# Quantizing the second weight of a two-layer kernel: one piece a tile over 32 tiles instead of two over 16, scaled on ScalarE

## The reference, cut to what matters

```python
x = x + _L0_ffn_ref(_L0_cond_ref(x, L0_cond_weights, itok_B_0_15), ...)   # first layer
x = x + _L1_ffn_ref(_L1_cond_ref(x, itok_B_6_15, ...), ...)               # second layer

# inside _L1_ffn_ref: both operands are rounded to float8 before the product
x_q = _quant_fp8(x, 1.0 / input_scale)
w_q = _quant_fp8(weight, 1.0 / weight_scale)      # weight: 1024 x 1024, (w * scale_inv).astype(float8_e4m3fn)
acc = jnp.einsum('ni,io->no', x_q.astype(jnp.float32), w_q.astype(jnp.float32))
out = acc * (input_scale * weight_scale) + bias
```

## Time and profile before

| | us |
|---|---|
| median of 3 runs | 2068.76 (2067.19 to 2071.76) |
| the profiled execution | 2070.12 |
| its span on the core | 2068.3 |
| PE busy in the span | 2022.6 (98%) |
| DVE busy | 1438.4 (70%) |
| POOL busy | 517.7 (25%) |
| ACT busy | 381.3 (18%) |

### The profile page before, as it was taken

How to read it: one execution, slowest core, us unless ns; L and a number is a source line. 1 busy time by engine, 2 the same in 40 slices (tenths; PEclk the granted TensorE clock), 3 DMA queues, 4 the chain that set the end, 5 groups by cost and what they waited for, 6 DMA issues and landing times.

```text
span 2068.3 us, 36401 instructions
## 1 busy us (share of the span) xinstructions
PE 2022.6 (98%) x11969; PEld 1898.7 (92%) x12032; DVE 1438.4 (70%) x3786; ACT 381.3 (18%) x1052; POOL 517.7 (25%) x470
## 2 busy tenths in 40 slices
PE   7998999999999999999999999999999999999998
PEld 6998999999999999999988888888888888888887
DVE  6798987555555555555557777777777777777777
ACT  3111111111111111111111221211211211211211
POOL 3654411111111111111112222222322322222322
PEclk8999999999999999999999999999999999999999
DMA  7753443333333333333354556556556556556553
GB/s 237 238 172 118 140 125 103 93 107 107 96 93 111 106 94 93 113 105 93 93 175 145 157 154 168 160 157 166 159 161 164 157 164 163 155 168 159 155 170 112
DMA packets 220193, 289.85 MB, mean 140 GB/s; under 512 B 97795, under 2 KB 169477, under 8 KB 220166
## 3 DMA queue, kind: packets, MB, share of 16 engines
q1 hardware_dynamic: 220166, 289.56, 48.4%
HBM read 163.62 MB, written 109.05 MB: 132 GB/s over the span
## 4 chain that ended last, share of the span: by engine, by line
PE 90%; DVE 7%; issue 1%; SPq 1%; DMA 1%; ACT 0%; DVEq 0%; ACTq 0%
PE bank_g L946 12%; PE bank_g L948 12%; PE bank_g L947 12%; PE bank_g L1000 12%; PE bank_g L999 12%; PE bank_g L998 11%; PE bank_f L1008 10%; PE bank_t L929 5%; PE bank_g L1043 1%; PE bank_g L973 1%; PE bank_g L974 1%; PE bank_g L975 1%; DVE hwt L317 1%; DVE wq_pow L751 1%; DVE x1buf L812 1%
## 5 line engine op out<-in xcount | busy, mean ns | idle before, releaser
L946 PE MATMUL bank_g<-w0h,st_h 128*128 128x384 f32 (+1 forms) x1536 | 525.5, 342 | 18.6 <-DVE x1buf L812 15.3
L948 PE MATMUL bank_g<-w0h,st_l 128*128 128x384 f32 (+1 forms) x1536 | 524.0, 341 | 0.0
L947 PE MATMUL bank_g<-w0l,st_h 128*128 128x384 f32 (+1 forms) x1536 | 523.7, 341 | 0.0
L998 PE MATMUL bank_g<-w1h,st_h 128*128 128x352 f32 x1536 | 506.6, 330 | 2.9 <-DVE st_l L863 2.5
L1000 PE MATMUL bank_g<-w1h,st_l 128*128 128x352 f32 x1536 | 497.3, 324 | 0.0
L999 PE MATMUL bank_g<-w1l,st_h 128*128 128x352 f32 x1536 | 496.4, 323 | 0.0
L863 DVE TENSOR_TENSOR st_l<-xbuf,st_h 128x512 fp32r<-128x512 f32 x128 | 213.2, 1708 | 186.6 <-ACT st_h L663 186.6
L552 POOL TENSOR_TENSOR xbuf<-xbuf,b_base_sb 128x1024 f32<-128x1024 f32 x64 | 153.7, 2402 | 704.2 <-PE bank_t L929 690.7
L946 PEld LDWEIGHTS bank_g<-w0h,st_h 128*128 128x128 f32 x1536 | 292.0, 190 | 21.7 <-DVE st_l L711 17.0
L998 PEld LDWEIGHTS bank_g<-w1h,st_h 128*128 128x128 f32 x1536 | 289.6, 189 | 11.0 <-DVE st_l L863 2.8
L947 PEld LDWEIGHTS bank_g<-w0l,st_h 128*128 128x128 f32 x1536 | 291.6, 190 | 0.0
(11 more groups left out here) (79 smaller groups left out, 2085.6 us busy)
## 6 DMA issues: line engine op xcount, KB each, us to landing
xbuf<-x SPq DMA_DIRECT2D x64, 512.0 KB, 3.8
x_scratch<-x1buf SPq DMA_DIRECT2D x64, 512.0 KB, 2.9
x1t_scratch<-x_blocks SPq DMA_DIRECT2D x256, 128.0 KB, 2.2
xbuf<-x1t_scratch SPq DMA_DIRECT2D x64, 512.0 KB, 3.6
x1buf<-x_scratch SPq DMA_DIRECT2D x64, 512.0 KB, 5.1
out<-obuf SPq DMA_DIRECT2D x64, 512.0 KB, 2.7
b_stack<-b_split SPq DMA_DIRECT2D x384, 64.0 KB, 3.5
raw<-a_split SPq DMA_DIRECT2D x128, 128.0 KB, 4.1
```

Of the source, the lines that this page charges most:

```text
L946: pe.matmul(to, st_h[:, rows], w0h[:, k, cols], start=(k == 0), stop=False)
L947: pe.matmul(to, st_h[:, rows], w0l[:, k, cols], start=False, stop=False)
L948: last = pe.matmul(to, st_l[:, rows], w0h[:, k, cols], start=False, stop=(k == KC - 1))
L998: pe.matmul(to, st_h[:, rows], w1h_k[:, k, cols], start=(k == 0), stop=False)
```

## The change

The number of pieces a tile goes from two to one, and the tiles that carry one are now 2 to 33; the piece stands at the end of VectorE's tile, after the transpose, and none before `st_lo(n, 0)`. The first of the seven instructions, the multiplication by `inv_w`, becomes a ScalarE instruction, in place in `wq_val`, after that tile's `st_hi`; VectorE waits for `wq_scaled`. SP's `feed(t)` no longer alternates: it feeds GpSimd's pieces first, and then reloads the weight's buffer for the piece of the tile before. The tiles written out grow from 18 to 34 for SP, GpSimd and VectorE; ScalarE's were written out for 2 and now are for 34.

```diff
-PREP_TILES = 18
-WQ_TILES = range(2, 18)
-WQ_A_TILE = 2
 WQ_COLS = 256
 WQ_PIECES = D * D // P // WQ_COLS
-WQ_STEPS = 7
+WQ_FIRST_TILE = 2
+WQ_STEPS = 6
+PREP_TILES = WQ_FIRST_TILE + WQ_PIECES
...
+def wq_piece(t):
+    return t - WQ_FIRST_TILE if WQ_FIRST_TILE <= t < PREP_TILES else None
...
                 def feed(t):
-                    quantized = [*wq_pieces(t - 1)[WQ_A_TILE - 1:], *wq_pieces(t)[:WQ_A_TILE - 1]]
-                    for n, u in zip_longest(pool_pieces(t), quantized):
+                    for n in pool_pieces(t):
                         feed_pool(n)
-                        feed_wq(u)
+                    feed_wq(wq_piece(t - 1))
...
-                tile(0, True)
-                tile(1, True)
-                with act.Fori(2, TILES - 3, 2) as i:
+                def scale_weight(u):
+
+                    act.wait_ge(wq_loaded[u % 2], 16 * (u // 2 + 1))
+                    val = wq_val[:, u % 2, :]
+                    act.activation(val, val, ACT.Copy, scale=inv_w[:, :]).then_inc(wq_scaled, 1)
+
+                for t in range(PREP_TILES):
+                    tile(t, True)
+                    if t == WQ_FIRST_TILE:
+                        act.wait_ge(s_scale, 3)
+                    if wq_piece(t) is not None:
+                        scale_weight(wq_piece(t))
+                with act.Fori(PREP_TILES, TILES - 3, 2) as i:
...
-                    dve.wait_ge(wq_loaded[u % 2], 16 * (u // 2 + 1))
-                    dve.tensor_scalar(val, val, inv_w[:, :], None, ALU.mult).then_inc(wq_step, 1)
-                    dve.wait_ge(wq_step, base + 1)
+                    dve.wait_ge(wq_scaled, u + 1)
                     dve.tensor_scalar(power.bitcast(U32), val.bitcast(U32), 0x7F800000, None, ALU.bitwise_and)\
                        .then_inc(wq_step, 1)
...
                     move_hw(dve.tensor_copy, 1)
-                    for u in wq_units[0:1]:
-                        quantize_weight(u)
-                    for u in wq_units[1:WQ_A_TILE - 1]:
-                        quantize_weight(u)
                     if more:
                         st_lo(n, 0)
...
-                    for u in wq_units[WQ_A_TILE - 1:]:
-                        quantize_weight(u)
+                    if piece is not None:
+                        quantize_weight(piece)
```

More of the change, by code:

```diff
@@ L14 @@
 from contextlib import ExitStack
-from itertools import zip_longest
 import numpy as np
@@ L62 @@
 OVERFLOW_C = float(np.float32(2.0 ** 127 / 235.0))
-PREP_TILES = 18
-WQ_TILES = range(2, 18)
-WQ_A_TILE = 2
 WQ_COLS = 256
 WQ_PIECES = D * D // P // WQ_COLS
-WQ_STEPS = 7
+WQ_FIRST_TILE = 2
+WQ_STEPS = 6
+PREP_TILES = WQ_FIRST_TILE + WQ_PIECES
 POOL_PIECES_A_TILE = 3
-def wq_pieces(t):
-    first = WQ_A_TILE * (t - WQ_TILES[0])
-    return range(first, min(first + WQ_A_TILE, WQ_PIECES)) if t in WQ_TILES else ()
+def wq_piece(t):
+    return t - WQ_FIRST_TILE if WQ_FIRST_TILE <= t < PREP_TILES else None
 def build(nc, x, ids0, ids1, wc, m0, b0, b_base, w1t, base_bias, a1, b1, wf, bias2, s_in, s_w, out):
@@ L205, in build @@
             wq_loaded = [sem(f"wq_loaded{b}") for b in range(2)]
+            wq_scaled = sem("wq_scaled")
             wq_step = sem("wq_step")
@@ L738, in quantize_weight, with tile @@
                     base = WQ_STEPS * u
-                    dve.wait_ge(wq_loaded[u % 2], 16 * (u // 2 + 1))
-                    dve.tensor_scalar(val, val, inv_w[:, :], None, ALU.mult).then_inc(wq_step, 1)
-                    dve.wait_ge(wq_step, base + 1)
+                    dve.wait_ge(wq_scaled, u + 1)
                     dve.tensor_scalar(power.bitcast(U32), val.bitcast(U32), 0x7F800000, None, ALU.bitwise_and)\
                        .then_inc(wq_step, 1)
+                    dve.wait_ge(wq_step, base + 1)
+                    dve.tensor_scalar(power, power, MIN_NORMAL, ROUND_C, ALU.max, ALU.mult).then_inc(wq_step, 1)
                     dve.wait_ge(wq_step, base + 2)
-                    dve.tensor_scalar(power, power, MIN_NORMAL, ROUND_C, ALU.max, ALU.mult).then_inc(wq_step, 1)
+                    dve.tensor_tensor(val, val, power, ALU.add).then_inc(wq_step, 1)
                     dve.wait_ge(wq_step, base + 3)
-                    dve.tensor_tensor(val, val, power, ALU.add).then_inc(wq_step, 1)
+                    dve.tensor_tensor(to, val, power, ALU.subtract).then_inc(wq_step, 1)
                     dve.wait_ge(wq_step, base + 4)
-                    dve.tensor_tensor(to, val, power, ALU.subtract).then_inc(wq_step, 1)
+                    dve.tensor_scalar(wq_nan, to, OVERFLOW_C, 0.0, ALU.mult, ALU.mult).then_inc(wq_step, 1)
                     dve.wait_ge(wq_step, base + 5)
-                    dve.tensor_scalar(wq_nan, to, OVERFLOW_C, 0.0, ALU.mult, ALU.mult).then_inc(wq_step, 1)
-                    dve.wait_ge(wq_step, base + 6)
                     dve.tensor_tensor(to, to, wq_nan, ALU.add).then_inc(wq_step, 1)
-                def tile(t, b, stored, blocks, more, wq_units=()):
+                def tile(t, b, stored, blocks, more, piece=None):
                     n = t + 1
@@ L822, in tile @@
                                   x1buf[:, b, :].rearrange("p (k q j) -> p k q j", q=4, k=KC)).then_inc(blocks_done, 1)
-                    for u in wq_units[WQ_A_TILE - 1:]:
-                        quantize_weight(u)
+                    if piece is not None:
+                        quantize_weight(piece)
                 for t in range(PREP_TILES):
-                    tile(t, t % 2, 16 * (t // 2) if t >= 2 else None, 64 * t if t else None, True, wq_pieces(t))
+                    tile(t, t % 2, 16 * (t // 2) if t >= 2 else None, 64 * t if t else None, True, wq_piece(t))
                 with dve.Fori(PREP_TILES, TILES - 3, 2) as i:
```

## The result

The changed kernel takes 2044.99 us (median of 4 runs, 2044.25 to 2045.61), the one before 2070.26 beside it (2067.19 to 2072.36). The ratio is 0.9875, with a 95% interval of 0.9863 to 0.9887: faster by 25.3 us. The profiled execution took 2044.62 us, its span is 2042.8, against 2070.12 and 2068.3.

The account below looks back on a forecast made before the run. PE bounds the kernel, losing time only to VectorE stalls and slow clock in tiles 2 to 17. Idle 15.3 plus slow clock 7.7 make 23.0 us, off 2068.76: 2045.8 us; range 2043.0 to 2054.0.

Parts of the forecast that it names:

- The sum: Tiles 2 to 17: 22.99 us excess goes, 15.3 of PE idle and 7.7 at the lower clock; nothing added on the path.
- The late piece: VectorE after the transpose: six steps put `negmax` at +5.7 or +6.4, `hwt` at +12.3 or +13.0 against +14.5; cost 0.
- the +7.9: Latest `negmax` after a tile's first bank matmul, 14.5 - 6.6; past it beside wide splits the prediction is wrong.
- its upper bound: Worst traced piece, tile 3's before `st_lo`, put late: `negmax` +8.1, `hwt` +14.7, 0.2 us late; under 1 us over four tiles.
- a fraction of a us: SP's `feed(t)` may pass 15.89 us by this in tiles 2 to 5; costed at 0, upper bound 1 us.
- Rival A: Full exclusion: late piece can't run beside any split, `hwt` 2.8 us late in four tiles; about 2059 us; whole or part 0.13.
- The stated slack: Room before `hwt` is needed at +14.5: 2.2 us beside narrow splits, 1.5 beside wide ones; PE waits for nothing.
- The scaling: Multiplication moved to ScalarE after `st_hi`: 0.42 us, result near +0, VectorE asks at +2.7; costs 0.
- the early piece: VectorE's piece ahead of `st_lo(n, 0)`, held to be what is late: 4.73 us in tile 9, 5.79 in tile 3; removed.
- The reading of L751: VectorE's L751 takes 2.34 us in tile 9 against 0.23 in tile 15, standing until GpSimd's bias addition ends.
- The added tiles: Tiles 18 to 33 gain a piece of 2.05 us, hidden before the first bank group ends at +4.8; cost 0.
- Rival C: SP's late weight reload holds ScalarE's scaling and the exponential behind it; at 1.0 us a tile, 2078 us; chance 0.04.

## Why the prediction was right, and where it wasn't

The predicted 2045.8 us lies 0.8 from the measured 2045.0, and the range held it. Part of that closeness is luck. The forecast takes 23.0 us off a median of 2068.76, and beside the changed kernel the kernel before took 2070.26: 23.0 us were forecast and 25.3 measured. That no tile stalls at all is also partly luck, as tile 6 shows below.

**The sum.** 22.99 us were to go between tiles 2 and 17; 22.95 went, idle and slow clock both. The rest of the 25.3 is behind the first layer and in the spread of the runs. That stretch took 1022.7 and 1022.5 us in the two profiles of the kernel before, and 1020.1 to 1022.4 in the eleven of the other kernels, all with the same second layer. The difference between two of those is nearly as large as what is to be explained. Part of it is the landing of one small transfer into `b_stack`, for which PE waited 1.95 us before and not at all after; but the runs with the longer piece and with the added wait, both below 1021.3, waited 1.96 and 2.04 for it. Another part is the clock: over the 80 us behind the last `cond` the mean granted clock is 0.96 in both profiles of the kernel before, and 0.98 to 1.00 in the other eleven. The prediction had named a change of the second layer's time as a sign that it is wrong, and there is one, of 2.7 us. Whether the change has a share in it is open; the prediction saw no cause, and the runs show none.

**The late piece.** `negmax` at +5.7 beside narrow splits was right (+5.8). Beside wide ones +6.4 was right for tiles 3 and 4 (+6.1 and +5.9) and wrong for 5 (+7.3), and tile 6, whose splits are narrow, has +8.1. That is past the +7.9 that the prediction named as a sign of being wrong beside wide splits, and it is its upper bound for `negmax` to the tenth; it had taken 0 and not that bound. Two steps failed. One is SP's: its backlog of "a fraction of a us" was costed at nothing because what it loads is early. But it delays GpSimd's splits, the splits delay the bias addition, and the addition then meets the late piece. The other is the price of six steps beside wide splits, "some 3.7", from one tile: the run with two splits a tile has 4.73 with no addition beside them. Rival A had the exclusion at the splits alone and for the whole piece. The runs show it step by step, at the splits and, longest, at the addition. The stated slack of 2.2 or 1.5 us was 0 in tile 6. It cost 0.04 us here. With pieces longer by 1.3 us, tile 6 alone lost 6.2 of the 8.3 us.

**The scaling.** 0.42 us was estimated, 0.50 measured, off the path as said. That it is worth little where it stands was true of the changed kernel (about 2 us, 2046.95 against 2044.99, of which 1.3 are in the tiles with splits). But alone it brings 21 of the 25 us, with two stalls left, in tiles 4 and 6. The prediction gave the whole gain to the early piece, and didn't add up VectorE's chain. That chain is, with the addition kept away, 15.8 us to `st_lo`, against 14.4. Without the scaling the early piece is 0.4 us shorter (171.42 - 169.38 = 2.04 after 177.78 - 175.34 = 2.44) and the late one, beside splits, 0.7; the chain of that kernel ends at +14.5 (171.42 less 156.88), a tenth from what is wanted. Taking the early piece out removes 2.4. From tile 8 on either is enough, and together they don't add.

**The lock.** The reading of L751 held: it starts 0.11 us after the addition and ends 0.09 us after it, and L749 stands in the same way in tile 6 of the changed kernel, until 0.15 us after the addition's end. The Trainium skill, "SBUF — State Buffer", section "SBUF: two separate sides", has the engine that starts first keep the shared port pair for its whole instruction, where the VectorE instruction is in a mode that uses two ports or has two inputs in SBUF. The rows of the addition agree (2.37 and 2.34 us for steps of 0.29 and 0.23); those of a split's first instruction don't, as the last section shows. `st_lo`, which has one of its inputs in `bank_t`, where TensorE writes, takes its usual 0.68 in tile 8 of the kernel with the scaling alone moved, where it starts at 171.42 and the addition at 171.61. The collision makes a small lateness large: `st_lo` would be 1.0 us late in tile 9 of the kernel before and is 3.3 late (202.21 less 184.51, against +14.4). Which tiles it strikes differs between two executions.

**The added tiles.** 714.90 us from tile 17 to the last `cond`, before and after, with 16 more pieces in it: 0, as costed. Rival C doesn't occur: ScalarE is never idle before its 32 scalings, so the reload of a piece is never waited for.

## What to carry to other kernels

Add up the fixed-order queue of the engine that is late, from the event that starts it to the one that another engine waits for, and compare that with the time available, before giving a stall to one instruction in it. Where two engines exclude each other, a small excess becomes a large one: an excess of 1.4 us cost 0.8 of idle time with the addition kept away, and one of 1.0 cost 2.7 where the piece ran into it. Then a cut of that size, in whatever place, brings nearly all of it back, and a kernel that still fits may have no slack left: look at the worst tile and not at the typical one.

## What the runs showed of the hardware

Twelve copies of 32 x 64 on VectorE take 2.39 us alone and some 3.5 beside a narrow split. They take 4.70 us when GpSimd's addition over 128 x 1024 begins among them, and 6.65 with splits before and behind it. In the 4.70 us one copy, of 0.19 us otherwise, takes 2.26: it stands until the addition, which takes 2.34, is over.

The splits' two instructions act differently. In tile 9 of the changed kernel L749 (0.29 us alone) ends where the second one ends, at 171.50:

```profile
170.73 0.92 DVE L749 TENSOR_SCALAR wq_pow<-wq_pow 128x256 f32<-128x256 f32 x1
...
170.44 1.06 POOL L560 TENSOR_TENSOR w1l<-raw,w1h 128x352 fp32r<-128x352 f32 x1
```

Beside the first one (L559, 133.66 to 134.75 in the run with the longer piece) no copy stands for the whole of it: they take 0.39, 0.19 and 0.40 us where 0.19 is usual, and beside the second one, from 134.83 to 135.81, one takes 0.85.

The same VectorE steps take a different time beside different GpSimd work: six steps take 2.09 us alone, 3.47 beside narrow splits, 4.73 beside two wide ones, and 5.81 when the addition is among them (tile 6). The granted clock fell to 1.2 GHz around or after a stall in three of five cases in the first profile of the kernel before, but not after the two stalls of 2.70 us in tiles 9 and 11.
